# An attention and feed-forward block: in the second half of the tokens VectorE takes over the subtraction of the softmax's maximum from GpSimd

## The reference

```
h = layernorm(x) * (1 + ca) + sa                  # sa, ca, ga, sb, cb, gb from silu(c) @ wmod
q, k, v = h @ wq.T + bq, h @ wk.T + bk, h @ wv.T + bv     # each (token, 32 heads, 16)
scores = einsum('bshd,bstd->bsht', q, k) / 4
probs = softmax(scores, axis=-1)
x = x + ga * einsum('bsht,bstd->bshd', probs, v)
h = layernorm(x) * (1 + cb) + sb
x = x + gb * (h @ kernel + bias + per-batch LoRA + shared LoRA)
```

## Time and profile before

| | |
|---|---|
| median of 3 runs | 227.9 us (226.96 to 230.95) |
| the profiled execution, its time | 227.78 us |
| the profiled execution, its span | 226.0 us |
| TensorE busy | 193.6 us, 86% |
| VectorE busy | 115.7 us, 51% |
| ScalarE busy | 95.4 us, 42% |
| GpSimd busy | 97.8 us, 43% |
| granted TensorE clock, mean | 0.955 |

### The profile page before, as it was taken

The page is one execution under the profiler, slowest core; times in us unless marked ns, Lnnn a source line. Parts: engine busy times, 40 slices in busy tenths (PEclk is TensorE's granted clock), DMA queues, the critical chain, the costliest instruction groups (busy, mean ns, idle before and its releaser), DMA issues.

```text
span 226.0 us, 3282 instructions
## 1 busy us (share of the span) xinstructions
PE 193.6 (86%) x1290; PEld 160.2 (71%) x1290; DVE 115.7 (51%) x180; ACT 95.4 (42%) x165; POOL 97.8 (43%) x66
## 2 busy tenths in 40 slices
PE   0399999399952999999999999599996399999995
PEld 0399978288832679888879889486594286777774
DVE  4800299854404293796003687907759066853231
ACT  4300710996240027826451769741388004344420
POOL 7000299059920001898009896462359900431000
PEclk9999999999995589999999999999999959999999
DMA  5999971159289303901999998942824730111111
GB/s 188 352 272 279 340 257 1 1 78 183 115 210 152 57 0 75 127 4 47 127 245 131 246 149 235 124 148 70 161 59 103 153 107 0 46 48 49 46 73 67
DMA packets 29904, 28.95 MB, mean 128 GB/s; under 512 B 16672, under 2 KB 21024, under 8 KB 29248
## 3 DMA queue, kind: packets, MB, share of 16 engines
q1 hardware_dynamic: 29888, 28.74, 56.6%
HBM read 17.20 MB, written 2.10 MB: 85 GB/s over the span
## 4 chain that ended last, share of the span: by engine, by line
PE 52%; POOL 12%; DVE 9%; DMA 8%; SPq 7%; issue 5%; ACT 4%; DVEq 0%
PE ps L968 8%; PE ps L976 8%; PE ps L977 7%; PE ps L978 7%; PE ps L995 6%; POOL steps L484 5%; POOL steps L491 4%; SPq L427 4%; DMA kern_nat<-in_L_ffn_kernel_dram 4%; PE ps L1097 3%; PE ps L1111 3%; PE ps L1149 3%; DMA wm_attn<-in_L_wmod_dram 3%; DMA b_lo<-tail_lo 2%; SPq L359 2%
## 5 line engine op out<-in xcount | busy, mean ns | idle before, releaser
L484 POOL TENSOR_TENSOR steps<-steps,rmax 128x1024 f32<-128x1024 f32 x8 | 15.3, 1921 | 25.7 <-DVE rmax L854 25.7
L454 POOL TENSOR_TENSOR hT_lo<-h_full,hT_hi 128x512 fp32r<-128x512 f32 x8 | 11.0, 1398 | 30.3 <-ACT hT_hi L574 30.3
L995 PE MATMUL ps<-silu,wm_attn 128*128 128x1 f32 x64 | 13.8, 352 | 9.4 <-DMA wm_attn<-in_L_wmod_dram 9.4
L995 PEld LDWEIGHTS ps<-silu,wm_attn 128*128 128x128 f32 x64 | 13.7, 332 | 9.4 <-issue 9.4
L545 POOL TENSOR_TENSOR xres<-xres,bias_bc 128x512 f32<-128x512 f32 x8 | 10.9, 1387 | 18.5 <-DVE xn L775 18.5
L582 ACT ACTIVATE k<-ps,b_col 128x512 f32<-128x512 f32 x8 | 8.9, 1198 | 21.6 <-PE ps L978 21.6
L854 DVE TENSOR_REDUCE rmax<-steps 128x32 f32<-128x1024 f32 x8 | 9.6, 1200 | 14.8 <-ACT steps L551 14.8
L491 POOL TENSOR_TENSOR steps<-steps,rinv 128x1024 f32<-128x1024 f32 x8 | 15.4, 1921 | 3.8 <-DVE rinv L864 3.8
L705 ACT ACTIVATE h_full<-ps,modc 128x128 f32<-128x128 f32 x32 | 12.0, 456 | 10.7 <-PE ps L968 10.7
L976 PE MATMUL ps<-kern_lo,h_hi 128*128 128x512 f32 (+1 forms) x36 | 14.1, 393 | 2.0 <-issue 2.0
L1058 PEld LDWEIGHTS ps<-diag,q 128*64 128x64 f32 x256 | 14.6, 192 | 1.3 <-issue 1.3
(11 more groups left out here) (130 smaller groups left out, 471.8 us busy)
## 6 DMA issues: line engine op xcount, KB each, us to landing
wm_next<-in_L_wmod_dram SPq DMA_DIRECT2D x3, 1024.0 KB, 8.1
x<-_attn_hidden_states_dram SPq DMA_DIRECT2D x8, 256.0 KB, 7.6
wm_attn<-in_L_wmod_dram SPq DMA_DIRECT2D x4, 512.0 KB, 7.5
diag<-k SPq DMA_DIRECT2D x16, 128.0 KB, 4.8
q<-q SPq DMA_DIRECT2D x16, 128.0 KB, 6.5
diag<-v SPq DMA_DIRECT2D x8, 256.0 KB, 6.3
xres<-_attn_hidden_states_dram SPq DMA_DIRECT2D x2, 1024.0 KB, 7.9
out_dram<-xres SPq DMA_DIRECT2D x7, 256.0 KB, 2.0
```

Of the source, the lines that this page charges most:

```text
L454: nc.gpsimd.tensor_tensor(hT_lo[k][:, c], h_full[:, c], hT_hi[k][:, c].bitcast(F32), ALU.subtract).then_inc(h_split, 1)
L484: nc.gpsimd.tensor_tensor(rows, rows, rmax[:, c % 2 * RCH:(c % 2 + 1) * RCH].unsqueeze(2).to_broadcast([P, RCH, H]), ALU.subtract).then_in ...
L995: ins = nc.tensor.matmul(dst[:, n * IC + c:n * IC + c + 1], wm_attn[:, c, n * P:(n + 1) * P], silu[:, 2 * IC + c:2 * IC + c + 1], start=Tr ...
```

## The change

For chunks 4 to 7, `row_max` on VectorE is followed at once by the subtraction, a tensor_tensor of 128x1024 with `rmax` broadcast along the rows, which raises `shifted`. Because it reads what the instruction before it on the same engine has written, VectorE waits for `max_ready` first. GpSimd's `shift_rows` is left out for these chunks; it only normalises, chunk after chunk. The first half is as before. The multiplication of `kern_nat` stays in front of the normalisations on GpSimd.

```diff
-            shift_rows(NCH)
-            for c in range(NCH + 1, 2 * NCH):
-                shift_rows(c)
-                normalise_rows(c - 1)
-            normalise_rows(2 * NCH - 1)
+            for c in range(NCH, 2 * NCH):
+                normalise_rows(c)
...
                 nc.vector.tensor_reduce(rmax[:, b * RCH:(b + 1) * RCH], s_rows[c // NCH][:, c % NCH], AX_X,
                                         ALU.max).then_inc(max_ready, 1)
+                if c >= NCH:
+                    dve.wait_ge(max_ready, c + 1)
+                    rows = s_rows[c // NCH][:, c % NCH]
+                    nc.vector.tensor_tensor(rows, rows,
+                                            rmax[:, b * RCH:(b + 1) * RCH].unsqueeze(2).to_broadcast([P, RCH, H]),
+                                            ALU.subtract).then_inc(shifted, 1)
```

## The result

The changed kernel takes 233.88 us (median of 4 runs, 232.25 to 234.19) against 229.09 us for the kernel before in the same comparison (4 runs, 226.96 to 230.95). The ratio is 1.0226, with a 95% interval from 1.0115 to 1.0338: the change makes the kernel slower, by about 2%. Its profiled execution took 233.99 us with a span of 232.2; that of the kernel before took 227.78 with 226.0.

What follows compares the result with a forecast made beforehand. The prediction took the chain of waits through GpSimd and VectorE before TensorE's return as the bound, with VectorE becoming it after the edit. It summed 227.78 + 2.2 (later kern_lo) + 2.8 (lower clock) = 232.8 us, range 229.0 to 235.5.

Steps and rivals of the forecast that it cites:

- the two terms: Second half: kern_lo starts 2.2 us later; TensorE's clock falls in the longer gap, costing 2.8 us.
- The hold: VectorE's subtractions wait for GpSimd's SBUF work: first about 4.6 us under kern_nat's multiplication, third 1.9, second and fourth 1.2.
- The schedule: Chunks 4 to 7: VectorE needs 5.0 us per chunk against GpSimd's 3.8, so kern_lo starts at 143.3, not 141.13.
- the wait that the edit brings: First subtraction, issued at 119.45, finds GpSimd multiplying kern_nat until 122.94; VectorE stands still for 3.5 us.
- Rival 2: Engines run side by side in the second half's softmax; kern_lo 2.0 us earlier, 225.8 us; chance 0.09.
- The clock: TensorE's gap before 143.93 grows from 2.8 to 5.0 us; half clock for 6.0 us afterwards costs 2.8 us.
- rival 3: TensorE's clock stays low longer after the gap, 9.1 us, costing 4.3 us: 234.3 us; chance 0.08.

Runs made afterwards that it cites:

- The clearings: Changed kernel with GpSimd's multiplication of kern_nat replaced by three clearings of the same tile: 227.65 us (one run).
- The pair without the multiplication: Changed kernel and kernel before, each with GpSimd's multiplication of kern_nat replaced by clearing 8 columns: 227.94 and 224.67 us.
- the subtraction from PSUM: Changed kernel, but VectorE takes maximum and subtraction of chunks 4 to 7 straight from PSUM, without ScalarE's copies: 226.51 us, ratio 0.971.
- The same delay by other means: Kernel before with two additional VectorE reductions of 128x1024 in front of kern_lo: 233.39 us, ratio 1.025.
- kern_lo later in the changed kernel: Changed kernel with kern_lo behind the eight combinations of the context banks instead of in front: 229.71 us, ratio 1.0042.
- multiplication moved: Changed kernel with GpSimd's multiplication of kern_nat behind the normalisation of chunk 4 instead of in front: 229.39 us, ratio 0.9994.
- the gap of 4.50 us: Changed kernel with VectorE subtracting in chunks 6 and 7 only, GpSimd in 4 and 5: 231.15 us, ratio 1.0038.

## Why the prediction was right

- *The time.* 232.8 us was forecast, 233.88 measured, within 229.0 to 235.5. The sum was made against 227.78; the medians of the kernel before were 229.1 to 230.6. So as a difference 5.0 us was forecast and 4.8 measured. The closeness of these figures is partly luck. The base of the sum was a favourable execution, which kept its clock in the gaps at 41 and 141 us, and the profiled execution after lost 1.3 us ahead of the change. What bears the forecast out are the two terms: 2.2 and 2.8 us forecast, 2.21 and 2.65 measured between the marks.
- *The hold.* 4.6 us for the first subtraction, 1.9 for the third, 1.2 for the others; 4.63, 1.97, 1.22 and 1.23 measured. Two exchanges beside it show its condition. An operand in PSUM shows that it takes two SBUF inputs on VectorE's side, as the earlier trace rows suggested. The clearings show that it takes reads on GpSimd's side; the forecast's own sentence said only that GpSimd "works on SBUF operands". The rule of the Trainium skill that was weighed (SBUF — State Buffer, section "Who interferes with whom") names reads, and the traces agree with it: the hold lasts for 3.4 us (4.63 instead of 1.22) as it did for about one in the rows before.
- *The schedule.* Maximum 4 to kern_lo was forecast as 25.1 us (118.19 to 143.3) and measured as 25.15. Each step's duration came out, so the sum did.
- *What the prediction left unclear* is which part of the 2.2 us is whose. It named the hold as "the wait that the edit brings" and counted 3.5 us of standing still. The pair without the multiplication shows that this hold costs the change nothing against the kernel before, which paid the same 3.38 us on GpSimd's queue. The loss is the length of VectorE's lane, 5.0 us per chunk against 3.8, together with the hold by the normalisation of chunk 4 (0.75 of the 2.21 us). But the holds are what stood between the change and a gain: with the subtraction from PSUM, where there is none, the relay is 1.64 us shorter than before. Rival 2 had put that at 2.0.
- *The clock.* Forecast: a fall, 6.0 us at half clock behind TensorE's return, 2.8 us lost. Measured: a fall, 5.65 us, 2.65 us lost. The same delay by other means brings 2.5. The bet was on a gap between one of 3.7 us and one of 6.6, in both of which it fell. The argument was thinner than it looked: the gaps of 3.4 and 2.8 us that had kept their clock in the trace lost it in others. So a gap of 5.0 us made the fall likely; the rows of the kernel before couldn't set a length at which it comes. That rival 3's longer low clock (9.1 us) didn't come is as forecast.
- *Not foreseen:* 1.3 us of the profiled span are lost in the first half, where nothing was changed and where the clock fell in this execution.

## What to carry to other kernels

Before work is moved to VectorE, count its inputs in SBUF and look at what GpSimd reads at that moment: an operand taken from PSUM, or a reading instruction of GpSimd moved by one place, decided here over 2 to 4 us. Compare the length of the lane per chunk on the new engine with that on the old one; an engine that is busy half of the time over the span can be the bound of a stage. And a delay in front of TensorE can have a price of its own: here 2.2 us of waiting cost 4.9. What stands on the chain without being needed by the next step (kern_lo) was the cheapest gain.

## What the runs showed of the hardware

GpSimd's clearings left VectorE's subtraction alone (1.24 us beside 5.6 us of clearings). But another kind of instruction doesn't get by them. In the kernel before, in VectorE's and GpSimd's order of time:

```profile
8.37 0.17 DVE L763 TENSOR_SCALAR mv<-mv 128x4 f32<-128x4 f32 x1
...
35.29 3.83 DVE L763 TENSOR_SCALAR mv<-mv 128x4 f32<-128x4 f32 x1
...
159.64 1.23 DVE L763 TENSOR_SCALAR mv<-mv 128x2 f32<-128x2 f32 x1
```

```profile
33.78 5.31 POOL L459 MEMSET diag<- 128x2048 f32 x3
...
159.57 1.27 POOL L534 TENSOR_TENSOR b_raw<-b_raw,gb_bc 128x512 f32<-128x512 f32 x1 [3.57 <-ACT b_raw L551]
```

A tensor_scalar of 4 columns, 0.17 us long at 8.37, ended at 39.12, just behind the last of three clearings (39.09), over two boundaries between them. In the trace of the changed kernel it took 3.40 us and again ended with the clearings (38.71 against 38.69). At 159.64 one of 2 columns ended with GpSimd's multiplication (160.87 against 160.84). It has one SBUF input like the maxima, which aren't held, and by these rows it is held by writes alone as well as by reads. That rests on where it ended; no run was made to test it. The reading instructions of GpSimd let VectorE in between two of them: at 172.25 and at 174.32, and in the run with the multiplication moved, where the two engines took turns. What decides whose turn it is wasn't tried.

TensorE's clock fell behind gaps of 2.84 us and 2.76 us (kern_lo later in the changed kernel; multiplication moved) for 3.4 us of low clock, and not behind one of 2.84 us (before). In these two it fell 1.6 and 1.1 us after TensorE had gone back to work, so a gap's price need not show in the gap. With the gap of 4.50 us it fell at TensorE's return and was low for 3.4 us; with those of 5.01 and 5.40 us it fell in the gap and was low for 6.8 and 6.7 us, 5.65 and 5.2 of them behind the return. At this place, gaps of 1.6 us and less cost nothing in any trace.
